# Grouping tokens by expert in the last layer of a four-layer conditional transformer, for three of four batches

## The chip, the cores and the metric

The kernel runs on one core of a Trainium2 chip. The metric is the device time of one launch in microseconds, the median of several runs. A profile of one execution gives the rows that this document reads.

## The reference

Four batches of N = 512 tokens, C = 288 channels, go through a rotation (layer L0, a matrix exponential) and then three transformer layers with 16 heads of 18 channels and a hidden width of FF = 1152. The first two have one MLP each. The last one has four experts; each token uses the two with the largest gate logits:

```python
xn = _modulate(_ln(x), sh_mlp, sc_mlp)
xf = xn.reshape(-1, C)
gate_logits = xf @ w_gate                                   # 288 x 4
topk_logits, topk_idx = jax.lax.top_k(gate_logits, TOP_K)   # TOP_K = 2
gates = jax.nn.softmax(topk_logits, axis=-1)
cw = jnp.sum(jax.nn.one_hot(topk_idx, NUM_EXPERTS, dtype=xf.dtype) * gates[..., None], axis=1)
hmid = jax.nn.gelu(jnp.einsum('tc,ech->eth', xf, w1) + b1[:, None, :], approximate=True)
eo = jnp.einsum('eth,ehc->etc', hmid, w2) + b2[:, None, :]
moe = jnp.einsum('te,etc->tc', cw, eo).reshape(B, N, C)
return x + g_mlp[:, None, :] * moe
```

As written, every expert computes every token, and `cw` is zero for the two that are not chosen.

## The kernel before

Everything is laid out by hand on one clock of *ticks* (`ticks()`, `TICKS`), the same list for all five engines. After an opening (rotation, conditioning vectors, a barrier `phase_over` for all engines) each layer has an attention stage of 16 steps of 8 ticks (`AT[l]`; step s holds four heads of batch s // 4, so 32 ticks a batch) and an MLP stage (`MT[l]`) of two ticks for each hidden tile. `items()` lists pieces of work as (tick, kind, layer, index, part); `agenda(engine)` hands each engine its list, moved by the offsets in `LAG` (POOL mostly one tick later). An engine runs its list strictly in order and waits on semaphores; a tick is an order, not a time. SP issues every DMA of the kernel, also in list order.

The MLP stage goes through *windows* of FT = 9 hidden tiles, a window being one batch under one expert. `hidden(l, s)` makes a tile of 128 hidden units for 512 tokens with `seven` matmuls (line 1696: the operands are split into a high part in fp32r and a low part, and seven products of chunks of 128 or 96 rows give full precision). `gelu_tile` (ACT, line 1556) writes `g32`, DVE splits it into `G` (lines 1322 and 1324), and `back` (line 1780) adds 12 matmuls for each tile into four PSUM banks. `finish` (DVE, lines 1143 to 1151) adds the bias, multiplies by the MLP's gate and, in the last layer, by the token's weight `cw` for the expert, and adds to `X`. G has three buffers, g32 two, the hidden tile's bank one; `back` of a tile runs two tiles behind its `hidden`. The last layer has 16 windows, expert by expert, four batches each.

Weights come in six *pieces* for each expert (three of w1, three of w2): `load_piece` on SP into one of two raw slots, `high_weights` on ACT (line 1354), `low_weights` on POOL (line 877). W1 and W2 of the experts alternate between two places. An expert's six pieces are spread over four windows.

The token's input to the MLP is made by `stats2` and `mean2` (DVE, then four small POOL instructions, lines 890 to 896), `scale` (ACT), and three `ln2` items: four transposes on PE into PSUM bank 7 (line 1820), two copies with scale and shift on ACT (lines 1519, 1520), the low part on POOL (line 928). Bank 7 is shared by all kinds in `ON_BANK`: each use waits until the one ahead has been read. `gate` makes the logits with 28 products of 4 columns, `choose` ranks them by six comparisons on DVE, `gexp` takes a power on POOL (line 969), `weigh` makes `cw`. In the last layer gates and choices stand in the first four windows. In attention each step ends with `out` (a transpose on DVE, then a product on POOL, line 933) and `turn` (a second transpose), each batch with four `proj` items (PE line 1844, DVE line 1272, an addition on POOL, line 939). Key scores are line 1735, their exponentials ACT's line 1545, values line 1749, query scores line 1717 and their maxima DVE's line 1133.

## Time and profile before

| | |
|---|---|
| median of 3 runs | 1902.89 us (1901.86 to 1903.12) |
| the profiled execution | 1896.54 us, its span 1894.1 us |
| granted TensorE clock, mean | 0.950 |
| PE busy | 1738.4 us (92%) |
| DVE, ACT, POOL busy | 1159.2, 914.4, 577.1 us |
| DMA | 116.49 MB, 61 GB/s over the span |

### The profile page before, as it was taken

How to read it: one execution, taken by the hardware profiler on the slowest of the kernel's cores; microseconds unless marked ns; L12 is line 12 of the kernel's file. 1: busy time of each engine (PE TensorE's matmuls, PEld its weight loads, DVE VectorE, ACT ScalarE, POOL GpSimd, SP SyncE). 2: the span in 40 equal slices, each digit the busy share in tenths (PEclk: the TensorE clock that was granted, in tenths of full speed). 3: DMA queues.
4: the chain of work that ended last, by engine and by line, in shares of the span. 5: the costliest groups of instructions: out<-in, count | busy, mean ns of one | idle time of the engine just before them, and what ended most of it. 6: DMA issues, size and time to landing. Idle time of an engine off the chain costs nothing.

```text
span 1894.1 us, 27931 instructions
## 1 busy us (share of the span) xinstructions
PE 1738.4 (92%) x9838; PEld 1141.3 (60%) x9838; DVE 1159.2 (61%) x2573; ACT 914.4 (48%) x1635; POOL 577.1 (30%) x567
## 2 busy tenths in 40 slices
PE   6775899998998889998899999999999999999998
PEld 2443444433796634443378764444388899999997
DVE  7863677773555667677436567777445645455454
ACT  2323476667354468675745247676733322222221
POOL 4432122214555323332435232222523301101000
PEclk9997699999999889899899999998999899999999
DMA  7202333331001222323100223333110000100000
GB/s 245 79 2 71 95 105 91 91 112 48 11 1 51 91 82 72 90 70 114 57 11 1 88 67 109 92 100 114 39 38 19 20 25 20 44 10 29 1 26 25
DMA packets 65866, 116.49 MB, mean 61 GB/s; under 512 B 9443, under 2 KB 25235, under 8 KB 65439
## 3 DMA queue, kind: packets, MB, share of 16 engines
q1 hardware_dynamic: 65728, 114.71, 19.6%
q8 instruction: 79, 1.29, 0.3%
q14 instruction: 59, 0.48, 0.1%
HBM read 83.46 MB, written 30.73 MB: 60 GB/s over the span
## 4 chain that ended last, share of the span: by engine, by line
PE 70%; DVE 10%; ACT 7%; issue 4%; DMA 4%; POOL 4%; SPq 2%; DVEq 0%; ACTq 0%; POOLq 0%
PE ps L1696 25%; PE ps L1780 15%; PE ps L1749 8%; PE ps L1735 7%; PE ps L1844 6%; PE ps L1717 5%; ACT Pr L1545 2%; DMA heads_t<-stage 2%; PE ps L1820 1%; DVE negmax L1133 1%; ACT HQ L1520 1%; DVE GT L1059 1%; ACT act L1519 1%; ACT xn L1441 1%; PE ps L1586 1%
## 5 line engine op out<-in xcount | busy, mean ns | idle before, releaser
L1133 DVE TENSOR_REDUCE negmax<-ps 128x1 f32<-128x512 f32 x768 | 488.3, 681 | 221.3 <-PE ps L1717 218.0
L1545 ACT ACTIVATE Pr<-ps 128x512 f32<-128x512 f32 x768 | 410.6, 602 | 208.3 <-PE ps L1735 208.0
L1556 ACT ACTIVATE g<-ps,b1col 128x512 f32<-128x512 f32 x216 | 148.2, 688 | 449.1 <-PE ps L1696 445.0
L1322 DVE CAST G<-g 128x512 fp32r<-128x512 f32 x216 | 122.8, 568 | 280.7 <-ACT g L1556 280.2
L1735 PE MATMUL ps<-QK 55*128 55x512 f32 x768 | 239.5, 515 | 33.4 <-ACT Pr L1545 25.2
L1780 PE MATMUL ps<-W2a,G 128*128 128x288 f32 x1728 | 263.4, 302 | 4.8 <-DVE rowt L1143 4.8
L1780 PEld LDWEIGHTS ps<-W2a,G 128*128 128x128 f32 x1728 | 247.9, 192 | 19.1 <-DVE G L1324 7.3
L1749 PE MATMUL ps<-Pr,V 128*32 128x512 f32 x1536 | 220.0, 646 | 0.0
L1717 PE MATMUL ps<-QK 54*128 54x512 f32 x768 | 196.6, 444 | 18.7 <-DVE negmax L1133 7.0
L1735 PEld LDWEIGHTS ps<-QK 55*128 55x128 f32 x768 | 92.2, 192 | 198.7 <-ACT Pr L1545 103.5
L1324 DVE TENSOR_TENSOR G<-g,G 128x512 fp32r<-128x512 f32 x216 | 170.4, 789 | 7.4
L1696 PE MATMUL ps<-HQ,W1a 128*128 128x512 f32 (+1 forms) x504 | 136.4, 411 | 7.4 <-ACT g L1556 5.9
L928 POOL TENSOR_TENSOR stage<-act,stage 126x512 fp32r<-126x512 f32 (+1 forms) x60 | 77.3, 1288 | 203.7 <-ACT stage L1537 165.1
L1780 PEld LDWEIGHTS ps<-W2b,G 128*128 128x128 f32 x864 | 123.5, 188 | 6.3
L1780 PE MATMUL ps<-W2b,G 128*128 128x288 f32 x864 | 126.9, 296 | 0.0
L1717 PEld LDWEIGHTS ps<-QK 54*128 54x128 f32 x768 | 96.1, 198 | 44.7 <-DVE negmax L1133 21.9
L1844 PE MATMUL ps<-WP,oT 128*128 128x288 f32 x384 | 121.1, 445 | 0.0
L928 POOL TENSOR_TENSOR HQ<-act,HQ 128x512 fp32r<-128x512 f32 (+1 forms) x54 | 69.6, 1288 | 136.3 <-ACT HQ L1520 123.1
L1696 PEld LDWEIGHTS ps<-HQ,W1a 128*128 128x128 f32 (+1 forms) x504 | 93.3, 194 | 28.9 <-ACT g L1556 8.2
L1844 PEld LDWEIGHTS ps<-WP,oT 128*128 128x128 f32 x384 | 70.1, 199 | 63.7 <-issue 31.0
L1696 PEld LDWEIGHTS ps<-WQ,HQ 128*128 128x128 f32 (+1 forms) x560 | 80.8, 197 | 41.9 <-issue 14.0
L1696 PE MATMUL ps<-WQ,HQ 128*128 128x288 f32 (+1 forms) x560 | 98.5, 317 | 7.9 <-ACT stage L1537 3.3
(221 smaller groups left out, 2241.1 us busy)
## 6 DMA issues: line engine op xcount, KB each, us to landing
QK<-heads_t SPq DMA_DIRECT2D x192, 144.0 KB
heads_t<-stage SPq DMA_DIRECT2D x96, 252.0 KB
QK<-heads_t SPq DMA_DIRECT2D x192, 72.0 KB
raw<-in_w SPq DMA_DIRECT2D x18, 432.0 KB
raw<-in_w SPq DMA_DIRECT2D x12, 576.0 KB
WA<-in_ada_w SPq DMA_DIRECT2D x3, 1728.0 KB
heads_t<-stage SPq DMA_DIRECT2D x24, 144.0 KB
QK<-W1a SPq DMA_DIRECT2D x192, 2.0 KB
```

What stands on the lines that cost most here:

```text
L928: pool.tensor_tensor(lo, act32[rows, h % 2, :], hi.bitcast(F32), ALU.subtract).then_inc(low_done, 1)
L1133: dve.tensor_reduce(negmax[:, m % 2, h, t:t + 1], ps[:, row_bank(l, s, i), :], AX, ALU.max, negate=True).then_inc(a_free, 1)
L1322: dve.tensor_copy(G[:, n % 3, 0, :], g32[:, n % 2, :]).then_inc(g_hi, 1)
L1324: dve.tensor_tensor(G[:, n % 3, 1, :], g32[:, n % 2, :], G[:, n % 3, 0, :].bitcast(F32), ALU.subtract).then_inc(g_lo, 1)
L1545: act.activation(Pr[:, t % 2, 2 * half + pair, :], ps[:, (16 * s + u) % 3, :], ACT.Exp, scale=SCALE).then_inc(b_free, 1)
L1556: act.activation(g32[:, n % 2, :], ps[:, hidden_bank(s), :], ACT.Gelu if l == 1 else ACT.Gelu_apprx_tanh, bias=b1col[:, e, s % FT:s % FT + ...
L1696: ins = mm(o, lhs(w, h, rows[w]), rhs(w, h, rows[w]), start=p == 0, stop=p == 6)
L1717: mm(ps[:, row_bank(l, s, i), :], QK[r:r + QROW, g, 0, pair, 128 * t:128 * t + 128], QK[r:r + QROW, g, 1, pair, :], start=True, stop=True) ...
L1735: mm(ps[:, k % 3, :], QK[r:r + QROW + 1, g, 1, pair, 128 * t:128 * t + 128], QK[r:r + QROW + 1, g, 0, pair, :], start=True, stop=True).the ...
L1749: ins = mm(ps[32 * i:32 * i + 32, 6, :], V[:, s // 4 % 2, t, c:c + 32], Pr[:, t % 2, i, :], start=t == 0, stop=t == TT - 1)
L1780: ins = mm(ps[:, t, 0:C], G[:, n % 3, x, 128 * t:128 * t + 128], W2[e % 2][:, w, ft, :], start=ft == 0 and p == 0, stop=ft == FT - 1 and p ...
L1844: ins = mm(bank[:, 0:C], oT[:, (STEPS * l + 4 * i + g) % 5, 128 * k:128 * k + 128], WP[:, g, :], start=g == 0, stop=g == 3)
```

## The change

In the last layer, the tokens of batches 0 to 2 (SEL = 3) are grouped by expert. Their modulated rows are written to DRAM (`tok_rows`, a region of 1536 rows for each expert) at the place that a running count gives them, twice each, once for each chosen expert. The windows then are tiles of 512 such rows: 3 x 512 x 2 = 3072 rows are six tiles, and rounding up for four experts makes at most GROUPED = 9. Which expert a tile belongs to is known at run time only (`table`, read by SP as register values), so every window loads all six pieces, and its bias rows, by a computed address. A tile is read back (`xg`), transposed (`lng`), and its result stored (`exp_rows`). At the end a gather fetches the two results of each token, and `merge` weights and adds them. The fourth batch is computed as before, under all four experts, in four more windows. `tok_rows` is filled with zeros in the opening. Core of the diff:

```diff
+LAST, SEL = LAYERS - 1, B - 1
+GROUPED = 2 * SEL + EXPERTS[-1] - 1
+WINDOWS = (B, B, GROUPED + EXPERTS[-1])
+REGION = SEL * N
+XROWS = (EXPERTS[-1] + 1) * REGION
+CW = C + 64
...
-        tiles = EXPERTS[l] * B * FT
+        tiles = WINDOWS[l] * FT
...
+def raw_slot(n):
+    return n % 2 if n < THREE else (n - THREE) % 3
...
+def choices(l, b):
+    if b == 1:
+        out += [(6, "setup", l, 0, 0), (12, "wg", l, 0, 0)]
+    if b == 2:
+        out += [(12 + t, "stats2", l, 0, t) for t in range(TT)] + [(17, "mean2", l, 0, 0)]
+        out += [(10, "modrow", l, 0, 0), (24, "mod", l, 0, 0)] + [(26 + c, "ln2", l, 0, c) for c in range(3)]
+        out += [(20 + t, "stats2", l, 1, t) for t in range(TT)] + [(26, "mean2", l, 1, 0), (28, "modrow", l, 1, 0)]
+        out += [(29, "gate", l, 0, 0), (31, "gturn", l, 0, 0), (33, "gexp", l, 0, 0), (34, "rank", l, 0, 0), (35, "weigh", l, 0, 0)]
+        out += [(36, "scatter", l, 0, 0)]
+    if b == 3:
+        out += [(2 + c, "ln2", l, 1, c) for c in range(3)] + [(11, "mod", l, 1, 0)]
+        out += [(13, "gate", l, 1, 0), (15, "gturn", l, 1, 0), (17, "gexp", l, 1, 0), (18, "rank", l, 1, 0), (19, "weigh", l, 1, 0)]
+        out += [(20, "scatter", l, 1, 0)]
+        out += [(t, "stats2", l, 2, k) for k, t in enumerate((8, 10, 12, 14))] + [(14, "mean2", l, 2, 0), (14, "modrow", l, 2, 0)]
+        out += [(19, "mod", l, 2, 0)] + [(19 + c, "ln2", l, 2, c) for c in range(3)]
+        out += [(22, "gate", l, 2, 0), (24, "gturn", l, 2, 0), (26, "gexp", l, 2, 0), (26, "rank", l, 2, 0), (27, "weigh", l, 2, 0)]
+        out += [(27, "scatter", l, 2, 0), (27, "table", l, 0, 0), (30, "xg", l, 0, 0)]
+        first = PIECE["w1", l, 0, 0]
+        out += [(t, "load", l, first + q, 0) for q, t in enumerate((0, 0, 5, 9, 13, 26))]
+        out += [(t, "split", l, first + q, 0) for q, t in enumerate((4, 7, 10, 25, 31, 32))]
...
+def grouped_window(l, v):
     out = [(4, "fin", l, v - 1, 0)] if v > 0 else []
+    if 0 < v <= GROUPED:
+        out += [(5, "store", l, v - 1, 0)]
     if v == 0:
+        out += [(0, "out", l, STEPS - 1, 0), (0, "turn", l, STEPS - 1, 0)]
+        out += [(0, "proj", l, B - 1, t) for t in range(TT)]
+        out += [(0, "lng", l, 0, c) for c in range(3)] + [(6, "slots", l, 0, 0), (2, "b2", l, 0, 0)]
+    if v == 1:
+        out += [(t // 2, "stats2", l, B - 1, t) for t in range(TT)] + [(2, "mean2", l, B - 1, 0)]
+        out += [(8 + c, "ln2", l, B - 1, c) for c in range(3)]
+    if v == 2:
+        out += [(2, "gate", l, B - 1, 0), (4, "gturn", l, B - 1, 0), (6, "gexp", l, B - 1, 0), (9, "weigh", l, B - 1, 0)]
+    if v == 4:
+        out += [(3, "gates", l, 0, 0)]
+    if v + 1 < WINDOWS[l]:
+        first = PIECE["w1", l, v + 1, 0]
+        out += [(t, "load", l, first + q, 0) for q, t in enumerate((-3, -2, -1, 8, 10, 12) if v > 0 else (2, 2, 3, 8, 10, 12))]
+        out += [(t, "split", l, first + q, 0) for q, t in enumerate((5, 7, 9, 12, 14, 16))]
+        out += [(9, "side", l, v + 1, 0)]
+    if v + 1 < GROUPED:
+        out += [(1, "xg", l, v + 1, 0)] + [(11 + 2 * c, "lng", l, v + 1, c) for c in range(3)]
+    for b in range(SEL):
+        if v == GROUPED + b:
+            out += [(8, "gather", l, b, 0), (14, "merge", l, b, 0), (16, "merge", l, b, 1)]
...
+            sp.dma_start(tok_rows.rearrange("(k p) c -> p k c", p=128),
+                         act32[:, 0, 0:CW].unsqueeze(1).broadcast_to([128, XROWS // 128, CW])).then_inc(zero_out, 16)
...
+            sp.wait_ge(zero_out, 16)
             phase_end(sp)
...
+                elif kind == "scatter":
+                    pool.wait_ge(zero_out, 16)
+                    pool.wait_ge(mod_done, i + 1)
+                    pool.wait_ge(idx_ready, i + 1)
+                    for t in range(TT):
+                        for r in range(2):
+                            pool.indirect_dma_start(tok_rows, bass.IndirectOffsetOnAxis(idx[:, i, t, r:r + 1], 0),
+                                                    MB[i // 2][:, t, :], None).then_inc(xs_out, 16)
+                    pool.wait_ge(xs_out, 16 * 2 * TT * (i + 1))
+                elif kind == "gather":
+                    pool.wait_ge(ys_out, 16 * GROUPED)
+                    pool.wait_ge(slots_ready, 1)
...
+                    for t in range(TT):
+                        for r in range(2):
+                            pool.indirect_dma_start(XG[r][:, t, 0:C], None, exp_rows,
+                                                    bass.IndirectOffsetOnAxis(yidx[:, i, t, r:r + 1], 0)).then_inc(yg_in, 16)
+                    pool.wait_ge(yg_in, 16 * 2 * TT * (i + 1))
...
+                dve.tensor_tensor(mb[:, :, :], xn[:, :, :], bc3(modr[:, 1, :], TT), ALU.mult).then_inc(dve_done, 1)
+                dve.wait_ge(dve_done, step())
+                dve.tensor_tensor(mb[:, :, :], mb[:, :, :], bc3(modr[:, 0, :], TT), ALU.add).then_inc(mod_done, 1)
...
-                    for t in range(TT):
-                        ins = seven(bank[:, 4 * t:4 * t + 4], lambda w, h, r: x[0:r, h, 128 * t:128 * t + 128],
-                                    lambda w, h, r: Wg[0:r, w, :], KROWS)
+                    ins = seven(bank[0:4], lambda w, h, r: Wg[0:r, w, :], lambda w, h, r: x[0:r, h, :], KROWS)
...
+                late = (what, l, s, u) == ("m", LAST, 0, 0)
+                if what == "m" and u == 0 and (EARLY if l < LAST else 0) <= s < tiles and not late:
                     hidden(l, s)
...
                 for key in todo[tick]:
                     work(*key)
+                if late:
+                    hidden(l, s)
```

Not shown: `rank` (ranks of the tokens in their regions, a dozen small instructions on DVE behind two or three narrow matmuls), `table` and `slots` (some 20 and 13 small DVE instructions, once each), `gturn` (four narrow matmuls), `merge` (8 + 2 DVE instructions), the SP functions for `xg`, `store`, `side`, `modrow` and `gates`, and the waits that each new reuse of a buffer needs. `lng` is like `ln2` with plain copies.

## Rows read from the trace of the kernel before

**Rows 1.** Stretches: busy us of PE, PEld, DVE, ACT, POOL; clock; DMA share, GB/s.

```profile
1253.00:1313.00 60.00, 57.69 (x323) 25.77 (x319) 44.73 (x77) 36.94 (x71) 12.76 (x12) 1.00 0.28 86
1313.00:1377.00 64.00, 59.01 (x282) 23.92 (x282) 31.48 (x61) 45.84 (x87) 27.61 (x25) 0.89 0.21 64
1377.00:1533.00 156.00, 147.87 (x827) 129.40 (x826) 80.77 (x224) 51.44 (x76) 49.45 (x36) 0.91 0.09 30
...
1538.50:1567.60 29.10, 29.10 (x172) 26.26 (x172) 14.63 (x27) 6.19 (x9) 0.00 (x0) 1.00 0.00 1
```

**Rows 2.** POOL's timeline (start, length in us, engine, line, operation): one split, four windows apart.

```profile
1577.15 3.02 POOL L877 TENSOR_TENSOR W1a<-raw,W1a 128x1152 fp32r<-128x1152 f32 x1 [46.56 <-ACT W1a L1354]
...
1693.48 3.02 POOL L877 TENSOR_TENSOR W1b<-raw,W1b 128x1152 fp32r<-128x1152 f32 x1 [46.56 <-ACT W1b L1354]
```

**Rows 3.** Timeline of the last window: its last hidden tile, and its end.

```profile
1880.42 1.77 PE L1696 MATMUL ps<-HMw,W1b 128*128 128x512 f32 x7
...
1887.50 1.36 DVE L1148 TENSOR_TENSOR rowt<-rowt,gbc 128x1152 f32<-128x1152 f32 x1
```

**Rows 4.** End of attention, and the projection behind it, in the timeline.

```profile
1378.03 1.07 PE L1749 MATMUL ps<-Pr,V 128*32 128x512 f32 x8
...
1382.09 1.05 POOL L933 TENSOR_TENSOR oTok<-oTok,rsum 128x512 f32<-128x512 f32 x1 [10.59 <-DVE rsum L1250]
...
1388.63 2.10 PE L1844 MATMUL ps<-WP,oT 128*128 128x288 f32 x8
...
1390.87 0.46 DVE L1272 TENSOR_TENSOR ptmp<-ps,agate 128x288 f32<-128x288 f32 x1 [3.11 <-PE ps L1844]
...
1391.48 0.81 POOL L939 TENSOR_TENSOR X<-X,ptmp 128x288 f32<-128x288 f32 x1 [2.58 <-DVE ptmp L1272]
```

**Rows 5.** Timeline and clock around the third choice of experts.

```profile
1462.69 3.80 PE L1696 MATMUL ps<-Wg,HQ 128*128 128x4 f32 x28
...
1467.00:1471.00 4.00, 3.11 (x9) 0.50 0.00 0
```

**Rows 6.** The last transposes before a window, and what the window waits for.

```profile
1493.40 0.60 PE L1820 MATMUL ps<-ident,xn 128*96 128x128 f32 x4
...
1497.06 1.87 PE L1696 MATMUL ps<-HMw,W1a 128*128 128x512 f32 x7 [1.48 <-POOL HMw L928]
...
1491.00:1495.00 4.00, 4.00 (x28) 1.00 0.35 113
```

**Rows 7.** Part of one choice of experts on DVE, in the timeline.

```profile
1426.07 0.54 DVE L1171 TENSOR_TENSOR wins<-lg 128x4 f32<-128x4 f32 x6
```

**Rows 8.** The opening: last early load, first instruction behind the barrier, DMA rate.

```profile
70.06 0.28 SPq L687 DMA_DIRECT2D raw<-in_b_qkv  x1
...
133.87 0.52 POOL L906 MEMSET HQ<- 2x512 f32 x1 [6.62 <-ACTq L597]
...
10.00:20.00 10.00, 5.08 (x44) 2.05 (x44) 7.63 (x44) 1.80 (x6) 3.91 (x6) 1.00 1.06 303
```

**Rows 9.** Groups of instructions from 1360 us to the end.

```profile
L877 POOL TENSOR_TENSOR W1b<-raw,W1b 128x1152 fp32r<-128x1152 f32 (+1 forms) x6 | 16.7, 2787 | 85.1 <-ACT W1b L1354 85.0
L877 POOL TENSOR_TENSOR W2b<-raw,W2b 128x864 fp32r<-128x864 f32 x6 | 12.7, 2121 | 46.4 <-ACT W2b L1354 46.3
L969 POOL TENSOR_TENSOR tmp<-euler,tmp 128x16 f32<-128x16 f32 x4 | 12.4, 3110 | 36.1 <-DVE tmp L1167 36.1
...
L928 POOL TENSOR_TENSOR HQ<-act,HQ 128x512 fp32r<-128x512 f32 (+1 forms) x6 | 7.7, 1286 | 9.5 <-ACT HQ L1520 9.3
...
L1519 ACT ACTIVATE act<-ps,ada 128x512 f32<-128x512 f32 (+1 forms) x12 | 9.5, 788 | 11.0 <-PE ps L1820 11.0
```

**Rows 10.** Landing of the output's transfers, from the DMA view.

```profile
out<-X SPq DMA_DIRECT2D x4, 576.0 KB, 3.0
```

**Rows 11.** A split of weights on POOL beside a cast on DVE.

```profile
1448.84 2.67 POOL L877 TENSOR_TENSOR W1b<-raw,W1b 128x1152 fp32r<-128x1152 f32 x1
...
1449.73 2.07 DVE L1322 CAST G<-g 128x512 fp32r<-128x512 f32 x1 [2.98 <-ACT g L1556]
```

More of the change, by code:

```diff
@@ L288 @@
 LAG = {
[L289 to L290 removed]
+    "PE": dict(ym=0, l0=0, ln1=0, ln2=0, qk=0, tok=0, v=0, max=0, proj=0, gate=0, gturn=0, rank=0, lng=0, warm=0),
+    "ACT": dict(ym=0, scale=0, root=1, ln1=0, ln2=0, lng=0, gate=0, qk=0, tok=0, max=0, split=0, bias=0, wg=0),
     "DVE": dict(add=0, inverse=0, stats1=0, stats2=0, mean1=0, mean2=0, v=0, proj=0, out=0, turn=0, warm=0, var=0, root=0, centre=0, fin=0,
[L292 to L293 removed]
+                gturn=0, weigh=0, rank=0, table=0, slots=0, merge=0, mod=0),
+    "POOL": dict(gexp=0, setup=0, scatter=0, gather=0, mean1=1, mean2=1, ln1=1, ln2=1, lng=1, qk=1, out=1, proj=1, tok=1, root=3, split=1, centre=1, fin=1, wg=1,
                  ones=0, vones=0),
[L295 removed]
+    "SP": dict(onerow=0, qk=2, max=1, place=0, load=0, wp=0, agate=0, mlpc=0, b2=0,
+               modrow=0, xg=0, store=0, side=0, gates=0),
 }
@@ L1845, in work @@
                                  start=g == 0, stop=g == 3)
+                elif kind == "gturn":
+                    pe.wait_ge(misc_free, MISC["gate", l, i, 0] + 1)
+                    for t in range(TT):
+                        ins = mm(bank[:, 4 * t:4 * t + 4], lgT[:, 128 * t:128 * t + 128], ident[0:4, 0:4], start=True, stop=True)
                 else:
```

554 lines of the change are left out of this document (438 added, 116 removed).

## The prediction

> **What bounds the kernel now.** I read the cores' clock and the forty slices of the page first: PE is busy through the whole last layer. Then busy time by stretch [rows 1]. In attention for the last layer's batches 2 and 3 (1253 to 1377 us) PE is busy 116.7 of 124 us; DVE is at 75% and then 49%, POOL at 21% and 43%. From 1377 to 1533 PE still has 148 of 156 us, and from there each window (nine hidden tiles and their products back, for one batch and one expert) is PE alone: 29.1 busy of 29.1 us. The POOL timeline gives the period: the same weight split of two experts, four windows apart, stands 116.33 us apart, so 29.1 us a window [rows 2]. The last window begins eight tiles of 3.23 us ahead of its last hidden tile at 1880.42, at 1854.6; its final scaling starts at 1887.50 [rows 3], 32.9 us after the window's start, and 6.6 us before the span's end at 1894.1. Attention ends with the last values product at 1379.1 [rows 4]. From there to 1854.6 are 475.5 us for 15 windows, which at 29.1 are 436.5: 39 us go to the projection of batch 3, transposes, four gates and slow clock. One such place is the third gate: 28 products of 4 columns take 3.80 us and the clock behind them is granted at 0.50, 1.2 GHz instead of 2.4 [rows 5].
>
> **What it removes.** Sixteen windows become 9 grouped and 4 dense: three fewer, 3 x 29.1 = 87 us of pure PE time, and the count is fixed in the program, so that this part cannot fail to happen. The gates of 28 narrow products, with their slow clock, go too.
>
> **Attention, +27 us.** I measure it to its last values product. The two hidden tiles that lay inside it leave: -3 (two of 1.77 us [rows 3]). For each of three batches PE gets 12 transposes (1.8 us [rows 6]), 7 gate products of full width (1.8, as a hidden tile [rows 3]), 16 narrow ones for turning and ranking (1), 4.6 in all. DVE gets a choice (six comparisons take 0.54 us [rows 7]; some 22 such instructions and six waits, 2.3), a ranking of a dozen (2), statistics (2) and two passes of 1408 elements for the modulation, at 1.36 us for 1152 [rows 3] 1.65 each: 10 us. In the second half of batch 2, DVE already has 22 of 30 us: +7 us, of which 4.6 are PE's. In batch 3 POOL sets the pace. A scatter is 8 indirect transfers, and POOL then waits until they land. No row shows an indirect transfer. Bounds: SP's issue of a plain one, 0.28 us [rows 8], and POOL's longest small instruction, the power at 3.11 [rows 9]; I take 1.1, as a POOL instruction on 128 rows takes 1.05 [rows 4]. With landing at 3.0 [rows 10] a scatter holds POOL 8 x 1.1 + 3 = 12 us (bounds 5 and 28). From tick 4 to the gate of batch 2 at tick 22 POOL has, in its order: scatter 12; three W1 lows 8.4; four low parts of ln2 5.2 [rows 9]; four additions of the projection 3.2, two oTok products 2.1 [rows 4]; the small statistics 2; one power 3.1; the second scatter 12: 48 us. DVE and POOL hinder each other: a cast that started under a split on POOL ran 2.07 us and ended only behind it [rows 11]; 5 more. The gate on PE waits for the low parts queued behind the second scatter, and PE's queue, the key scores with it, stands behind the gate. 18 ticks of 64/32 = 2.0 us are 36: 53 - 36 = +17. Behind it gate, turn and rank on PE, exposed with few scores beside them: +3 and, for DVE's choice ahead of the rank, +3.
>
> The Trainium skill (DMA: Bandwidth & Descriptors, Anatomy of one DMA — SWDGE (gpsimd) path) has a fixed 2.0 us and bytes at 436 GB/s for a transfer of this path, 2.3 us for one of 180 KB; by that, an estimate, a group would end 0.7 us sooner and the six groups 4 us in all. No row here shows one.
>
> **The gap, 31 us.** Window 0's hidden tile now stands behind everything of its tick. Scatter 2 starts some 11 us behind gate 2 and ends at 23; two W2 lows (4.2) and the oTok product come behind it, at 28.5, while attention ends some 18 us behind that gate: 10 us late. Then the turn 0.7; four projections, each half of 2.10, 0.46 on DVE and hand-offs, 1.9 x 4 = 7.6 [rows 4]; three groups of transposes through one bank, 0.6 [rows 6] + 2 x 0.79 on ACT [rows 9] + 0.2, 7.1; a low part 1.3; and 4 for a clock at 0.50 once PE has idled, as [rows 5] shows behind light work. Bounds 20 and 45.
>
> **Windows, +24, +10, +9 us.** Eight windows hold 12 transposes more, 1.8 us. The last low part must be there when the next window begins: before, with transposes one tick later, PE waited 1.48 us [rows 6]; now a W2 low (2.1 [rows 9]) can stand ahead of it. I take 1.2 (bounds 0 and 3.6): 8 x 3.0 = 24. Each window now splits six pieces: 3 x 2.79 + 3 x 2.12 = 14.7 us, low parts 3.9, on POOL, and DVE, busy for 14.6 in a window [rows 1], has some 10 us of casts and differences that get in POOL's way: 28.6 of 32, it fits without much room. ACT needs 6.2 more of 32. Weights and tiles are 4.3 MB a window, 137 GB/s, under half the 303 that rows show [rows 8]: hidden. Batch 3's ln2, its gate and the scales of windows 1 and 2 are 10. Windows 9 to 11 each hold a gather of 12 us on POOL between two W1 lows; the piece of W2 whose slot the late low frees comes 8 us late, ACT waits for it ahead of the next gelu, and DVE's merge waits for the gather. A tile's G is ready some 2 us behind the tile and used two tiles, 6.5 us, behind it: against that slack of 4.5, 3 a window: 9 (bounds 0 and 45). Stores, side loads and table reads are SP's, with windows of time: nothing; if a table read blocked SP for 3 us, the W2 loads' 6 us lead would still cover it.
>
> **The opening, 0.** 7680 rows of 1408 bytes, 10.8 MB, are zeroed behind the last early load at 70.3, and SP's barrier waits for them; the barrier opens at 133.9 [rows 8]. That is 63.6 us, enough from 170 GB/s on. The opening's rate was 303, attention's 86 [rows 1]; I take 200. Bounds 0 and 62.
>
> **The sum.** 1379.1 + 27 + 31 = 1437.1; 12 x 29.1 = 349.2; + 24 + 10 + 9: the last window begins at 1829.3; + 32.9 + 6.6 = 1868.8, against 1894.1: 25 us less. The profiled execution took 1896.5 (its span and 2.4 around it), 6 us under the median of the runs, 1902.9; I put the difference on that: 1902.9 - 25 = 1878 us.
>
> **Rivals.** (a) The groups hide. If an indirect transfer costs POOL what it costs SP, a group is 5 us; POOL catches up in attention (+9), the gap is 21, transposes alone remain (14), windows 1 and 2 cost 7 and gathers nothing: 1379.1 + 9 + 21 + 349.2 + 14 + 7 + 39.5 = 1818.8, 75 less: 1828 us. POOL's 21 and 43% of busy time speak for it, the pile of splits and scatters in batch 3 against.
> (b) Slower: POOL's price for an indirect transfer. Eight of them count in two scatters, the late third and three gathers, 48 us for each us of price. It decides from 1.1 + 25/48 = 1.6 us on; at 2.2 it is +53, 1931 us. The 3.11 us for a power on 16 elements [rows 9] speaks for it, POOL's 1.05 us for 512 elements against.
> (c) The zeros at attention's rate: 62 us later, 1940.
> (d) The clock. The stretch that held the last transposes before a window was granted 1.00 [rows 6]. If the clock fell instead in each grouped window for some 8 us, as it does behind a gate of narrow products, at half speed that would be 4 us in each of eight windows: 1878 + 32 = 1910. The Trainium skill (TensorE: Matmul & The Clock Gate, Part 4: PE-mode transpose) says that transposes do not count as PE being busy as other matmuls do; by that rule (d) would come, and the trace does not bear it out.
>
> **Chances.** My forecast 0.53 (its own range 1848 to 1900), (a) 0.15, (b) 0.18, (c) 0.04, (d) 0.04, and 0.06 that extra waits eat the gain to within some us of nothing. A measurement here can tell 0.2%, 3.8 us. Faster: 0.53 + 0.15 + 0.02; slower: 0.18 + 0.04 + 0.03 for half of (d) and a share of the last; same 0.05. The range runs from (a) to short of (b)'s middle: 1828 to 1915; it leaves out the far half of (b), (c) and a little below (a).
>
> **What would show it.** In the profile of the changed kernel: POOL's time per indirect transfer (1.1 us) and per group (12); PE's wait at batch 2's gate for POOL's low part (over 8 us); about 31 us from the last values product to the first hidden tile; a grouped window of 32 us, a dense one 29 to 32; the first instruction behind the barrier still near 134; the clock at 1.00 in grouped windows. Wrong it is made above all by the price of an indirect transfer, by a barrier later than 140, or by ACT held at a W2 piece in every window.

## The result, and the profile after

The changed kernel takes 1927.2 us (median of four runs), the kernel before 1902.4: a ratio of 1.013, 95% interval 1.010 to 1.016. The forecast was 1878 us, 1828 to 1915. The profiled execution's span is 1920.3 us, 26.2 more than before, where 25 less were forecast: 51.5 us to account for.

The windows view of the changed kernel: attention from the ninth step's maximum to the last values product, in two parts; the gap to the first hidden tile; window 0 up to its first bias addition; windows 1 to 8; windows 9 to 11.

```profile
1249.40:1301.20 51.80, 51.80 (x288) 23.60 (x284) 39.89 (x77) 32.71 (x63) 13.46 (x16) 1.00 0.30 91
1301.20:1436.60 135.40, 101.50 (x426) 40.71 (x422) 71.72 (x218) 67.96 (x123) 66.63 (x57) 0.71 0.24 76
1436.60:1468.30 31.70, 15.03 (x44) 9.26 (x44) 3.51 (x7) 3.25 (x6) 13.04 (x12) 0.66 0.35 110
1468.30:1510.90 42.60, 39.03 (x199) 33.45 (x200) 28.15 (x42) 17.70 (x24) 20.62 (x11) 0.88 0.27 81
1510.90:1763.50 252.60, 248.97 (x1481) 222.14 (x1480) 173.67 (x202) 124.11 (x174) 155.67 (x76) 1.00 0.45 139
1763.50:1887.50 124.00, 99.74 (x515) 87.11 (x514) 91.56 (x108) 35.73 (x45) 67.06 (x42) 0.88 0.37 110
```

Up to 1301 hardly anything has changed (51.5 us before). Then the stretch that took 78.3 us takes 135.4: PE's busy time is up from 71.0 to 101.5, its idle time from 7.3 to 33.9, and the mean clock is down from 0.91 to 0.71. Grouped windows run at the full clock (1.00), as [rows 6] had it. Windows 9 to 11 take 124 us where three windows at 29.1 [rows 2] are 87: PE is idle for 24.3, and the same products take 99.7 us at a mean clock of 0.88.

What PE waits for in the second of these stretches (releaser: us in total, times, longest):

```profile
PE ps L2141 <- issue: 13.6, 2, 11.3
PE ps L2162 <- DVE negmax L1384: 9.1, 5, 2.7
PE ps L2194 <- DVE oTok L1647: 4.5, 2, 2.3
```

The timeline around the first of these, the gate of batch 2, then attention's end and the projection (start, length, engine, line, operation, idle time before it and what ended it):

```profile
1402.59 0.96 POOL L1203 DMA_INDIRECT tok_rows<-MB,idx  x1 [0.30 <-issue]
1405.17 2.59 POOL L1144 TENSOR_TENSOR HQ<-act,HQ 128x512 fp32r<-128x512 f32 x2 [1.62 <-DMA tok_rows<-MB,idx]
...
1407.86 3.15 PE L2141 MATMUL ps<-HQ,Wg 128*4 128x512 f32 x7 [11.27 <-issue]
...
1434.63 1.93 PE L2194 MATMUL ps<-Pr,V 128*32 128x512 f32 x8 [1.18 <-ACT Pr L1984]
1445.68 4.18 PE L2307 MATMUL ps<-WP,oT 128*128 128x288 f32 x8 [9.12 <-DVE oT L1655]
...
1468.34 3.36 PE L2141 MATMUL ps<-HQ,W1a 128*128 128x512 f32 x7 [2.62 <-POOL HQ L1144]
```

POOL issues the last transfers of batch 1's scatter, waits 1.62 us for them to land, and only then makes the low parts that the gate product needs: the gate has stood for 11.27 us and every key score behind it. An indirect transfer costs 0.96 + 0.30 us, a scatter 11.5 to 12.6 us with its landing (1.1 and 12 forecast). From 1400.2 to 1454.8 the clock is at 0.50, its lower level of 1.2 GHz: a values product takes 1.93 us and the projection 4.18, where [rows 4] has 1.07 and 2.10; the first window's hidden tiles take 3.36 against 1.77 [rows 3].

Window 9, on POOL and DVE:

```profile
1785.14 2.80 POOL L1093 TENSOR_TENSOR W1a<-WP,W1a 32x1152 fp32r<-32x1152 f32 x1 [1.93 <-DMA XG<-exp_rows,yidx]
1788.02 4.12 POOL L1093 TENSOR_TENSOR W2a<-raw,W2a 128x864 fp32r<-128x864 f32 x2
1792.34 2.00 POOL L1093 TENSOR_TENSOR W2a<-WP,W2a 128x864 fp32r<-128x864 f32 x1 [0.21 <-ACT W2a L1765]
1808.34 2.71 POOL L1093 TENSOR_TENSOR W1b<-raw,W1b 128x1152 fp32r<-128x1152 f32 x1 [14.00 <-ACT W1b L1765]
1811.56 2.73 POOL L1093 TENSOR_TENSOR W1b<-raw,W1b 128x1152 fp32r<-128x1152 f32 x1 [0.51 <-ACT W1b L1765]
...
1785.09 7.21 DVE L1422 TENSOR_SCALAR XG<-XG,cws 128x288 f32<-128x288 f32 x4 [5.29 <-DMA XG<-exp_rows,yidx]
1792.34 3.61 DVE L1426 SCALAR_TENSOR_TENSOR XG<-XG,cws,XG 128x288 f32<-128x288 f32 x4
...
1808.00 6.62 DVE L1408 SCALAR_TENSOR_TENSOR X<-rowt,cw,X 128x288 f32<-128x288 f32 x4
```

The gather holds the low parts back; the merge waits 5.29 us for it at the head of DVE's queue, and both then start together. DVE's four scalings take 7.21 us and end at 1792.30, 0.16 behind POOL's two W2 low parts; the finish's four accumulations take 6.62 and end at 1814.62, 0.33 behind its second W1 part. Experiment 3 shows such four beside an idle POOL at 1.81. PE waits 21.4 us for G in these windows, in five pieces.

### The profile page after: what moved, and what is told of

Read it like the earlier page. It is cut to its first block, busy times and chain, and to the rows that moved or that the text cites. A ratio compares the mean times of both kernels' runs of the same rounds, so it can differ in the third digit from the quotient of the medians.

```text
span 1920.3 us, 27798 instructions
## 1 busy us (share of the span) xinstructions
PE 1697.5 (88%) x9395; PEld 1079.3 (56%) x9395; DVE 1236.0 (64%) x2552; ACT 978.1 (51%) x1720; POOL 794.4 (41%) x713
## 4 chain that ended last, share of the span: by engine, by line
PE 59%; DVE 12%; ACT 8%; POOL 8%; issue 6%; DMA 4%; SPq 2%; another core or an unknown queue 0%; DVEq 0%; ACTq 0%; POOLq 0%
PE ps L2141 20%; PE ps L2229 10%; PE ps L2194 8%; PE ps L2180 7%; PE ps L2307 6%; PE ps L2162 4%; DMA heads_t<-stage 2%; ACT Pr L1984 2%; DVE negmax L1384 2%; PE ps L2283 1%; POOL W2a L1093 1%; DVE XG L1422 1%; POOL HQ L1144 1%; DVE GT L1310 1%; ACT HQ L1959 1%
## 5 line engine op out<-in xcount | busy, mean ns | idle before, releaser
L1997 ACT ACTIVATE g<-ps,b1col 128x512 f32<-128x512 f32 x189 | 129.7, 687 | 318.1 <-PE ps L2141 283.9
L1731 DVE CAST G<-g 128x512 fp32r<-128x512 f32 x189 | 142.4, 754 | 205.5 <-ACT g L1997 195.4
L2180 PE MATMUL ps<-QK 55*128 55x512 f32 x768 | 241.5, 528 | 26.5 <-ACT Pr L1984 18.3
L2229 PE MATMUL ps<-W2a,G 128*128 128x288 f32 x1620 | 245.1, 301 | 8.1 <-DVE G L1733 7.5
L2229 PEld LDWEIGHTS ps<-W2a,G 128*128 128x128 f32 x1620 | 231.7, 191 | 21.4 <-DVE G L1733 10.0
L2162 PE MATMUL ps<-QK 54*128 54x512 f32 x768 | 199.7, 447 | 29.3 <-DVE negmax L1384 16.2
L2141 PE MATMUL ps<-HQ,W1a 128*128 128x512 f32 (+1 forms) x693 | 189.6, 414 | 15.2 <-ACT g L1997 8.9
L1733 DVE TENSOR_TENSOR G<-g,G 128x512 fp32r<-128x512 f32 x189 | 194.6, 1030 | 6.5
L2180 PEld LDWEIGHTS ps<-QK 55*128 55x128 f32 x768 | 93.1, 196 | 186.3 <-ACT Pr L1984 91.1
L2141 PEld LDWEIGHTS ps<-HQ,W1a 128*128 128x128 f32 (+1 forms) x693 | 129.9, 197 | 45.7 <-ACT g L1997 12.6
L1144 POOL TENSOR_TENSOR HQ<-act,HQ 128x512 fp32r<-128x512 f32 (+1 forms) x69 | 90.8, 1315 | 142.0 <-ACT HQ L1959 117.6
L2307 PE MATMUL ps<-WP,oT 128*128 128x288 f32 x384 | 126.3, 461 | 11.5 <-DVE oT L1655 9.1
L2162 PEld LDWEIGHTS ps<-QK 54*128 54x128 f32 x768 | 96.6, 200 | 57.2 <-DVE negmax L1384 33.9
L2229 PE MATMUL ps<-W2b,G 128*128 128x288 f32 x648 | 98.8, 303 | 13.9 <-DVE G L1733 13.9
L1149 POOL TENSOR_TENSOR oTok<-oTok,rsum 128x512 f32<-128x512 f32 x48 | 50.8, 1059 | 140.9 <-DVE rsum L1649 140.0
L2229 PEld LDWEIGHTS ps<-W2b,G 128*128 128x128 f32 x648 | 94.8, 194 | 20.5 <-DVE G L1733 15.9
## 6 DMA issues: line engine op xcount, KB each, us to landing
tok_rows<-act SPq DMA_DIRECT2D x1, 10560.0 KB, 34.5
```

The costliest lines, as they stand in the source:

```text
L1144: pool.tensor_tensor(lo, act32[rows, h % 2, :], hi.bitcast(F32), ALU.subtract).then_inc(low_done, 1)
L1731: dve.tensor_copy(G[:, n % 3, 0, :], g32[:, n % 2, :]).then_inc(g_hi, 1)
L1733: dve.tensor_tensor(G[:, n % 3, 1, :], g32[:, n % 2, :], G[:, n % 3, 0, :].bitcast(F32), ALU.subtract).then_inc(g_lo, 1)
L1997: act.activation(g32[:, n % 2, :], ps[:, hidden_bank(l, s), :], ACT.Gelu if l == 1 else ACT.Gelu_apprx_tanh, bias=b1col[:, v % 4 if l == L ...
L2141: ins = mm(o, lhs(w, h, rows[w]), rhs(w, h, rows[w]), start=p == 0, stop=p == 6)
L2162: mm(ps[:, row_bank(l, s, i), :], QK[r:r + QROW, g, 0, pair, 128 * t:128 * t + 128], QK[r:r + QROW, g, 1, pair, :], start=True, stop=True) ...
```

## The experiments

All are variants of the changed kernel. Beside them the kernel before was run again, on four chips: medians of 1898 to 1902 us, and each ratio is against these runs. What lies ahead of attention's last part is the same code in all of them and still ends up to 14 us apart, so stretches are compared inside each execution: **attention** is from the ninth step's maximum to the last values product (before 129.8, changed 187.2), the **gap** from there to the first hidden tile (changed 31.8), **windows 9 to 12** from the first bias addition of window 8 to that of the last (changed 148.5; the last four before 111.7). Each stretch is read from one execution. The seven kernels with the change's attention (the change, 3 to 6, 8 and 9) took 185.5 to 190.9 us for it, so a difference under some 3 us there says nothing; the gap was 31.8 in six of them.

**1. Batch 1's scatter two steps later.**

```diff
-        out += [(20, "scatter", l, 1, 0)]
+        out += [(22, "scatter", l, 1, 0)]
```

> The change with one edit: batch 1's scatter, whose eight indirect transfers hold GpSimd for 12.6 us, is queued two steps later, behind the low parts that batch 2's gate product waits for. Theory 1 (the new queue order on GpSimd): TensorE no longer waits 11.3 us before that gate product, its clock does not fall to 0.50 around it, attention's last values product comes 15 to 25 us earlier than 1436.6, the gap after it and the first window (both run at half clock in the change) get shorter by another 5 to 15 us, and the whole is 1895 to 1905 us. Theory 2 (attention is late because VectorE is overloaded by the choices' small operations): the wait moves from GpSimd to VectorE's row maxima, the end of attention moves by less than 5 us and the whole stays at 1920 to 1927.

Measured: 1917.9 us, 1.0094 [1.0064, 1.0124]. The wait of 11.3 us is gone, attention takes 182.1: 5 us less. Its clock is still 0.81 on average (0.79 in the change), and PE now waits for DVE:

```profile
PE ps L2162 <- DVE negmax L1384: 11.6, 5, 3.7
PE ps L2194 <- DVE oTok L1647: 4.8, 1, 4.8
```

Theory 1 falls as the main cause; theory 2 is nearer, though the wait is real.

**2. One transfer of eight in a scatter.**

```diff
-                    for t in range(TT):
-                        for r in range(2):
+                    for t in range(1):
+                        for r in range(1):
                             pool.indirect_dma_start(tok_rows, ...
```

> The change with only the first of the eight indirect transfers of each scatter issued, so seven eighths of the tokens' rows are left out of the grouped computation; everything else, the zero fill and all the loads among it, stays. GpSimd is free 10.5 us earlier at each of the three scatters. Theory 1 (GpSimd's occupation by the scatters sets attention's end): last values product near 1410 instead of 1436.6, the gap of 31.8 us shorter by 3 to 6 us because the sixth W2 low part and the last output's scaling come sooner, whole 1888 to 1900. Theory 2 (VectorE's load): end of attention near 1430, whole 1918 to 1925. Windows 9 to 11 are as in the change under both, 41 us each.

Measured: 1914.1 us, 1.0060 [1.0024, 1.0095]; attention 174.7, gap 27.7. Eighteen us less of POOL's time in attention gave 12.5, half of what theory 1 wanted, and more than theory 2 allowed.

**3. Gather at step 17, merge at steps 2 and 3 of the next window.**

```diff
-            out += [(8, "gather", l, b, 0), (14, "merge", l, b, 0), (16, "merge", l, b, 1)]
+            out += [(17, "gather", l, b, 0)]
+        if v == GROUPED + b + 1:
+            out += [(2, "merge", l, b, 0), (3, "merge", l, b, 1)]
```

> The change with the three gathers issued from the seventeenth step of their window, behind the window's last low part, in place of the eighth, and the merges at steps 2 and 3 of the next window, ahead of its first low part. Theory 3 (in windows 9 to 11 GpSimd's twelve microseconds for a gather push the low parts back, and the merge then collides with them): windows 9 to 12 take 120 to 128 us in place of 148.5, whole 1898 to 1908. Rival (the merge's own arithmetic on VectorE, 7 to 9 us of it a window beside G's, is what the windows are longer by): 136 to 146 us, whole 1915 to 1924. Attention and the gap stay as in the change.

Measured: 1949.3 us, 1.0231 [1.0163, 1.0300], windows 9 to 12 163.9. Neither held, because I had put the merge ahead of the finish (step 4) that frees PSUM. DVE waits for the gather at the head of its queue (32.5 us in the three windows), and PE for DVE:

```profile
1816.83 3.56 DVE L1424 TENSOR_SCALAR XG<-XG,cws 128x288 f32<-128x288 f32 x4 [10.95 <-DMA XG<-exp_rows,yidx]
...
1829.09 1.81 DVE L1410 SCALAR_TENSOR_TENSOR X<-rowt,cw,X 128x288 f32<-128x288 f32 x4
```

**4. No weighting in the merge.** Nine of its ten operations are gone.

> The change with the merges' weighting left out: the gathered rows of the first choice are added to X as they are, the two scalings by the choice's weights, the second choice's rows and the product with the gate row are left out (of ten VectorE operations a merge one stays). Gathers and their places stay. Theory 3 (GpSimd's occupation by the gather decides): windows 9 to 12 take 138 to 146 us in place of 148.5, whole 1917 to 1925. Rival (the merge's arithmetic on VectorE decides): windows 9 to 12 take 118 to 126 us, whole 1897 to 1907.

Measured: 1915.6 us, 1.0076 [1.0043, 1.0108]; windows 9 to 12 132.3. That is 16.2 us less for 3 x 5 us of unhindered work, between the two expectations: the merge decides nearly half of the excess.

**5. Merge at steps 9 and 11 of the next window**, gather as in 3.

> The change with each gather issued from step 17 of its window, as in the third experiment, but the merges at steps 9 and 11 of the next window, behind the finish of step 4, so that VectorE never waits for a gather in front of the bias additions that free PSUM. Theory 4 (an SBUF operation of VectorE starts only between GpSimd's big operations, and a gather waited for at the head of VectorE's queue stops everything behind it; the third experiment was slower because TensorE waited 16 us three times for the bias additions): windows 9 to 12 take 120 to 138 us in place of 148.5 (163.9 in the third experiment), and the merge's ten operations still take 8 to 14 us in windows 10 and 11, but about 6 in window 12, where GpSimd has no low parts. Rival (the gathers' time on GpSimd alone decides): 142 us or more.

Measured: 1915.8 us, 1.0067 [1.0033, 1.0101]; windows 9 to 12 128.3. The scalings still took 18.5 us for twelve where they met low parts.

**6. Low parts of 64 columns for windows 3 to 12.**

```diff
+                if PIECES[n][0] == "w2" and PIECES[n][2] >= 3:
+                    lo, part, high = lo[:, 0, 0:64], part[:, 0, 0:64], high[:, 0, 0:64]
+                elif PIECES[n][0] == "w1" and PIECES[n][2] >= 3:
+                    lo, part, high = lo[:, 0:64], part[:, 0:64], high[:, 0:64]
```

> The change with GpSimd's low parts of the weights cut to 64 columns for windows 3 to 12 of the last layer (the other columns of the low part are left as they were, so the last bits of these products are not computed); high parts, gathers and merges stay. Theory 4 (VectorE's operations wait for GpSimd's): windows 9 to 12 take 115 to 125 us in place of 148.5, the merge's four scalings take 1.5 us in place of 7.2, the last window's four accumulations 1.8 in place of 6.6; windows 4 to 8 go from 31.0 to 29.1. Rival (the gather's landing and VectorE's own work decide): windows 9 to 12 stay above 136 us, windows 4 to 8 at 31.0.

Measured: 1895.8 us, 0.9977 [0.9934, 1.0019]; windows 9 to 12 114.5, with gathers and merges where the change has them. The groups of DVE in these windows, of the change and then of this kernel (count, busy us, mean ns of one, idle before):

```profile
L1422 DVE TENSOR_SCALAR XG<-XG,cws 128x288 f32<-128x288 f32 x12 | 19.4, 1673 | 5.3 <-DMA XG<-exp_rows,yidx 5.3
L1408 DVE SCALAR_TENSOR_TENSOR X<-rowt,cw,X 128x288 f32<-128x288 f32 x12 | 15.0, 1314 | 0.1
L1731 DVE CAST G<-g 128x512 fp32r<-128x512 f32 x34 | 18.3, 538 | 35.8 <-ACT g L1997 26.4 <-issue 9.2
```

```profile
L1426 DVE TENSOR_SCALAR XG<-XG,cws 128x288 f32<-128x288 f32 x12 | 4.7, 454 | 9.7 <-DMA XG<-exp_rows,yidx 9.7
L1412 DVE SCALAR_TENSOR_TENSOR X<-rowt,cw,X 128x288 f32<-128x288 f32 x12 | 5.6, 529 | 0.1
L1735 DVE CAST G<-g 128x512 fp32r<-128x512 f32 x34 | 14.4, 425 | 30.6 <-ACT g L2001 30.4
```

The same twelve scalings take 4.7 us in place of 19.4, though DVE now waits longer for the gathers (9.7 us) than before. The gathers' time alone costs next to nothing. The edit frees POOL as well as DVE; what PE waited for in the change's windows 9 to 11 was DVE's G (21.4 us), and no wait there is put down to POOL. Windows 4 to 8 went only from 31.0 to 30.4: of the 1.9 us over 29.1, 1.3 stay with the transposes and 0.6 were POOL's (in the change PE waits 0.3 us in such a window for the late low part).

**7. Less choosing on DVE** (for batches 1 and 2 the comparisons are skipped, batch 1 is modulated for one tile of four).

> The change with less of the choices' work on VectorE: for batches 1 and 2 the twenty small operations that find the chosen experts are left out (batch 0's choices are used again), and the modulated rows of batch 1 are made for one tile of four. That is some 6 us less of 72 us of VectorE's work in the last batch of attention. If VectorE's load is what makes TensorE wait and its clock fall, attention's last values product comes 12 to 25 us sooner, counted from the ninth step's maximum (187 us in the change, 130 before). If it is GpSimd's queue, it comes less than 5 us sooner.

Measured: 1918.1 us, 1.0077 [1.0048, 1.0105]; attention 178.4, mean clock 0.85. Six us of DVE's work were worth 9, between the two; the gate's wait of 11.4 is still there. PE's idle time did not change (34.3 us for 33.9): the 9 us came back as busy time (144.1 for 153.3) at the higher clock.

**8. Eight idle products on PE behind attention's last.**

```diff
+                    if l == LAST:
+                        filler(8)    # mm(ps[:, 5, 0:288], ident, V[:, 1, 0, 0:288])
```

> The change with eight products of 128 by 288 that compute nothing used, queued on TensorE behind attention's last values product, where it waits 9.1 us for VectorE and GpSimd. If the half clock of the projections and of the first window comes from TensorE's idle time just before, the projections take 2.1 to 2.3 us in place of 4.18, and from the last values product to the first window's first bias addition it takes 60 to 66 us in place of 74.4. If the clock does not depend on it, or the fillers only hold the projections up, 74 to 79 us. Everything ahead and behind is as in the change.

Measured: 1932.1 us (two runs), 1.0150 [1.0036, 1.0265]; from the last values product to the first bias addition 73.6 us (74.4 in the change). The clock rose at 1446.0 and fell again at 1452.8: the first projection took 2.84 us in place of 4.18, the second 4.21 as before. The gain that was expected did not come. Between the fillers and the first projection PE still waited 3.19 us for DVE, and 0.65 behind it; which pause brought the clock down again is not shown.

**9. Merges and finishes in two-operand forms.**

```diff
-                    for t in range(TT):
-                        dve.tensor_scalar(XG[0][:, t, 0:C], XG[0][:, t, 0:C], cws[:, b, t, 0:1], None, ALU.mult)...
+                    for r in range(2):
+                        y = XG[r][:, :, 0:C]
+                        dve.tensor_tensor(y, y, cws[:, b, :, r:r + 1].broadcast_to([128, TT, C]), ALU.mult)...
```

> The change with the merges and the finishes of windows 9 to 12 written in two-operand operations alone: a tile's scaling by a column (four operations with a scalar for each tile) becomes one product of 128 by 1152 with that column broadcast, and one sum. Order, places and gathers stay. In the change, in windows 9 to 12, VectorE's operations of those forms were 29.0 us longer than their shortest ones in sum (those of L1422 15.8, of L1408 9.7, of L1426 3.5), while the two-operand ones of L1405, L1433 and L1435 kept their 1.35 us. Theory 5 (only the forms with a scalar operand and the one-operand casts wait for GpSimd's operation in flight): windows 9 to 12 take 122 to 134 us in place of 148.5. Rival (every form waits; the long two-operand ones only happened to run beside an idle GpSimd): 144 to 154 us, and the new products take 2 to 4 us each.

Measured: 1935.8 us (two runs), 1.0171 [1.0119, 1.0222]; windows 9 to 12 152.3. Theory 5 falls. Two groups of this kernel, the merge's product and the finish's:

```profile
L1423 DVE TENSOR_TENSOR XG<-XG,cws 128x1152 f32<-128x1152 f32 x6 | 17.1, 2891 | 6.0 <-DMA XG<-exp_rows,yidx 6.0
...
L1408 DVE TENSOR_TENSOR rowt<-rowt,cw 128x1152 f32<-128x1152 f32 x3 | 4.1, 1358 | 0.1
```

The same product takes 2.89 us in the merge and 1.36 in the finish. The form doesn't matter, the neighbour does, and who came first: two of the finish's three products began 0.35 and 0.63 us ahead of a low part, kept their 1.36, and the low part took 3.54 and 3.27 us in place of 2.7. The sum behind each began inside the low part and took 3.7.

**10. Scatter as in 1, the table behind the last output's transpose, the last output scaled by DVE.**

```diff
-        out += [(0, "out", l, STEPS - 1, 0), (0, "turn", l, STEPS - 1, 0)]
+        out += [(0, "out", l, STEPS - 1, 0), (0, "table", l, 0, 0), (0, "turn", l, STEPS - 1, 0)]
```

> The change with three moves out of GpSimd's and VectorE's queues in attention's last stretch: batch 1's scatter two steps later as in the first experiment; the table of the windows' starts (4.2 us of small operations on VectorE before attention's end) made after the last output's transpose; and the last output's scaling done by VectorE, where it stood on GpSimd behind the third scatter and two low parts (7.2 us of VectorE's wait at 1437.6). Theory: the gap of 31.8 us becomes 24 to 28, attention's last values product comes 5 to 12 us sooner after the ninth step's maximum than the 187 us of the change, whole 1903 to 1913. Rival (GpSimd's low parts and the clock bound the gap, VectorE's table was hidden): gap 30 to 32, attention 182 to 184, whole 1916 to 1922.

Measured: 1916.8 us, 1.0081 [1.0049, 1.0113]; attention 177.1, gap 30.3. Attention did better than the rival said, the gap and the whole as the rival said; experiment 16 tells why the gap did.

**11 and 12. The moves of 10 and 5 together**, with the forms of 9 and with the old ones.

> The change with the moves of the tenth experiment, the gathers and merges of the fifth (gather at step 17, merge at steps 9 and 11 of the next window) and the two-operand forms of the ninth. If the gains add, 187 minus 5 to 12 for attention, gap 24 to 28, windows 9 to 12 120 to 128 us: whole 1878 to 1895 us, 0.99 to 1.00 of the kernel before. If attention's clock gives the gains back, 1895 to 1905.

> The eleventh experiment with the merges and finishes in their old forms (one operation with a scalar for each tile). If the forms did not matter, or the broadcast products cost a little more: windows 9 to 12 128 us (130.5 in the eleventh, 128.3 in the fifth), attention 177 to 179 us from the ninth step's maximum, gap 30, whole 1893 to 1899 us.

Measured: 1898.0 us, 0.9979 [0.9948, 1.0010], and 1897.6 us, 0.9977 [0.9947, 1.0008]; windows 9 to 12 130.5 and 128.3, attention 178.5 and 177.9, gap 30.3 in both. The gains of 5 and 10 add. The whole lies where the second expectation of 11 had it, level with the kernel before, because the gap had not shrunk; 12 came as expected.

**13. Low parts in thirds.**

> The twelfth with GpSimd's low parts of the weights for windows 2 to 12 made in three operations of a third each (384 columns, or one block of 288) in place of one. Theory 4 (an SBUF operation of VectorE waits for the one that GpSimd has in flight): the longest wait falls from 2.5 us to about 1, so VectorE gets in more often; windows 9 to 12 120 to 126 us in place of 128, whole 3 to 8 us less than the twelfth. Rival (only the sum of GpSimd's time counts, and it grows by some fixed cost for each operation): 128 to 133 us, no gain or a loss.

Measured: 1909.0 us, 1.0026 [0.9995, 1.0058]. The longest wait of a scaling fell from 2.5 us to 0.9, but windows 9 to 12 took 127.3 and windows 1 to 8 262.6 in place of 252.6. The rival holds: shorter waits, as long a sum (DVE is busy for 91.1 us of windows 9 to 12, 92.4 in experiment 12), and more work for POOL (78.9 us for 70.7).

**14. The cuts of 2 and 7 on top of 12.**

> The twelfth with the cuts of the second and of the seventh experiment together: one of eight transfers a scatter, the twenty choosing operations of batches 1 and 2 and three quarters of batch 1's modulation left out. If attention's lateness is VectorE's load, GpSimd's occupation and the clock that falls with TensorE's waits, and nothing else, from the ninth step's maximum to the last values product it takes 150 to 163 us (187 in the change, 177 in the tenth, 130 before). If something else makes TensorE late (its own added work, the spills), it stays at 168 or more.

Measured: 1884.7 us, 0.9893 [0.9847, 0.9938]; attention 162.3, mean clock 0.87. It is at the upper end of what the loads should explain: 25 of the 57 us. PE is busy for 142.5 us of it, 122.5 before. Of the 32.5 us that are left over the kernel before, 12.5 are idle time of PE and 20.0 busy time; by groups the added products, less the hidden tiles and the old gate, are 16 of the 20.

**15. The modulated rows made by GpSimd**, on top of 12.

> The twelfth with the three batches' modulated rows made by GpSimd in place of VectorE: 12.8 us less on VectorE in attention's last stretch, 16 to 20 more on GpSimd. If VectorE's load decides, attention takes 165 to 173 us from the ninth step's maximum in place of 177 to 179, whole 1885 to 1893. If GpSimd's queue decides as much (two operations of 2.7 to 3.5 us each ahead of the low parts), 177 to 188 us, whole 1895 to 1908.

Measured: 1889.6 us, 0.9945 [0.9919, 0.9971]; attention 174.7. For attention this is less than the first expectation gave and better than the second; the whole is in the first one's range. DVE and POOL at step 18 of batch 3:

```profile
1385.70 3.16 POOL L1129 TENSOR_TENSOR MB<-xn,modr 128x1408 f32<-128x1408 f32 x1 [0.29 <-ACT xn L1868]
1388.93 3.21 POOL L1131 TENSOR_TENSOR MB<-MB,modr 128x1408 f32<-128x1408 f32 x1
```

```profile
1387.11 1.78 DVE L1467 TENSOR_SCALAR pen<-chosen 128x16 f32<-128x16 f32 x1
1388.92 3.25 DVE L1471 TENSOR_TENSOR seen<-place_in,pen 128x16 f32<-128x16 f32 x2
```

An operation on 16 elements takes 1.78 us and ends within 0.04 us of POOL's; the next two take 3.25 and end with POOL's second. At 1413.08 to 1413.37, beside POOL's power on 16 elements, the latter two take 0.29.

**16 and 17. The table behind the turn; then gathers and merges moved away from low parts.**

```diff
+            out += [((17, 21, 0)[b], "gather", l, b, 0)] if b < 2 else []
+        if (v, b) == (GROUPED + 1, 0):
+            out += [(17, "merge", l, 0, 0), (18, "merge", l, 0, 1)]
+        if (v, b) == (GROUPED + 3, 1):
+            out += [(1, "merge", l, 1, 0), (3, "merge", l, 1, 1)]
+        if (v, b) == (GROUPED + 3, 2):
+            out += [(5, "gather", l, 2, 0), (15, "merge", l, 2, 0), (16, "merge", l, 2, 1)]
```

> The fifteenth with the table made after the last output's turn in place of ahead of it. In the fifteenth VectorE had the output scaled at 1426.2 and began its turn only at 1433.4, behind the table's small operations, three of which took 1.9 to 2.2 us beside GpSimd's two low parts. Theory: the table's 4 to 7 us now lie beside the first projection (4.0 us), the gap of 30.1 us becomes 23 to 27, whole 1881 to 1887, 0.990 to 0.993 of the kernel before. Rival: the table holds the first projection's product with the gate row up by what it held the turn up before, the gap stays at 28 to 30.

> The sixteenth with gathers and merges moved to where GpSimd has no low parts in flight: gather of batch 0 at step 17 of window 9, its merge at steps 17 and 18 of window 10, gather of batch 1 behind it (it lasts into window 11 and holds that window's low parts up by some 8 us), its merge at steps 1 and 3 of the last window, which has no low parts, gather of batch 2 at step 5 and its merge at 15 and 16. Theory 4 (merges are slow only beside low parts): windows 9 to 12 take 116 to 122 us in place of 128, whole 6 to 12 us less than the sixteenth. Rival: the low parts held up in window 11 make TensorE wait at the start of window 12, or the last merge comes late to the end: 124 to 132 us, no gain.

Measured: 1890.4 us, 0.9959 [0.9933, 0.9984], gap 27.7; and 1888.7 us, 0.9934 [0.9911, 0.9957], gap 27.7 and windows 9 to 12 124.9. In 16 the last output's turn starts 1.8 us behind its transpose (in 15 8.9 us), but the table, beside the two low parts, now ends at 1439.25; the second projection waits 3.29 us for it and then takes 4.21 us in place of 2.21, at the lower clock: two thirds of the 7 us are lost again. Its gap is just under the rival's range, its whole above what was expected. In 17 windows 9 to 12 came as the rival said, with 1.7 us less in all where 6 to 12 were expected. The merge's scalings are down to 5.4 us for twelve, but the low parts have moved onto G's casts instead (26.0 us for 34, 18.3 in the change):

```profile
L1744 DVE CAST G<-g 128x512 fp32r<-128x512 f32 x34 | 26.0, 766 | 25.6 <-ACT g L2010 25.4
...
L1446 DVE TENSOR_SCALAR XG<-XG,cws 128x288 f32<-128x288 f32 x12 | 5.4, 512 | 0.0
```

It is the fastest of those that compute everything: 0.7% under the kernel before, some 2% under the change by the two ratios. The intervals of 15, 16 and 17 overlap.

## Why the prediction was wrong

The miss by place: attention 30.5 us (57.5 for +27), the gap 0.8, window 0 6.6 (42.6 from its first hidden tile to its first bias addition; in the kernel before, the window before the last begins at 1825.5 and has its at 1861.5, 36.0), windows 1 to 8 14.2 the other way, windows 9 to 12 27.8 (148.5 less 111.7 is 36.8, for 9). The two large ones have causes of their own.

**"Windows, ... +9": the gathers' term, mis-sized (36.8 us for 9).** I had weighed the late W2 piece against PE's slack and let the merge wait for the gather. What I left out is the merge and the finish themselves beside the low parts. I had the row for it, [rows 11], and used it for attention ("5 more"); for the windows I added DVE's work to POOL's and found that "it fits" in POOL's 32 us, without asking the same of DVE. While POOL subtracts a piece of weights, DVE's casts, scalings and two-input operations on SBUF wait for its end. In a window, by [rows 9] and [rows 1], 14.7 us of POOL's pieces and some 10 of DVE's casts and differences already exclude each other for 25 of 29 us; the finish adds 3.2 and a merge 6.1 (experiment 6), and the window overflows. That sum, 34 us, tells that it overflows and not by how much: of the 36.8 us, 24.3 are PE's idle time and 12.4 the same products at a clock of 0.88. Experiment 6 shows the cause: with small pieces the excess goes from 36.8 us to 2.8 with every gather and merge in place. The Trainium skill (SBUF — State Buffer, Who interferes with whom) says this of a VectorE operation in a two-port mode or with two SBUF inputs against a GpSimd one that reads SBUF: an exclusive lock, held for the whole instruction, for whoever comes first. These rows agree for POOL's subtractions, sums and products, with 1.78 us for 16 elements and 1.67 in place of 0.45 for a scaling. They do not for its power, which held no operation of DVE's (last section); there the measurement decides. I had cited nothing of it in the prediction, where it would have named the missing sum. Experiment 9 shows that it is not the form, 13 that it is not the length of one piece, and 4, 5 and 17 give back 16 to 24 us by taking merges out or away from the pieces.

**"Attention, +27": a bound left out.** The chain that I named is there: POOL 11.3 us late at batch 2's gate, scatters of 12 us (12 forecast), and PE's queue stands behind it. But it was not the bound: with the wait gone (experiment 1) PE waits for DVE's row maxima and output transposes, and 5 us come back. I had counted DVE's 10 us a batch in the second half of batch 2, and for batch 3 only POOL's, as if POOL were full; from 1345 to the gate it was idle for 10.6 us for DVE alone (5.6 for the projection, 5.0 for the statistics). There DVE's work went from 42.6 to 71.7 us, nearly all of the 78.3 that the stretch had taken, in one queue with the maxima for which PE waits. Then the clock: I gave it 4 us in the gap and none in attention. PE, which had waited 7 us, waited 34, and the clock's mean over attention went from 0.95 of 129.8 us to 0.79 of 187.2. So the 57.4 us are 26.6 of idle PE and 30.8 of busy PE. Of the busy time some 20 are the added products by their groups (transposes 9.1 for 2.0, gates 9.1, turns 4.0, ranks 4.2, less 3.8 for the hidden tiles and 0.4 for the old gate), where the forecast's 4.6 a batch less 3 is 10.8; a gate of 1.8 us took up to 3.15 at the lower level. The other 10 are mostly the same products more often at half clock (the 260 values products 43.4 us for 37.3, the 94 query products 24.2 for 21.2). Shown by runs: the gate's wait (5 us), the scatters (12.5), DVE's work (9), both with the moves (25). The other 32 are read from experiment 14's rows (16 added products, 4 the same ones, 12.5 waits) and not taken away by any run. What brings the clock down stays open too: experiment 7 had as much idle time as the change and a mean of 0.85 for 0.79, and experiment 8's attempt in the gap gained nothing.

**Rival (d)** had its place wrong: grouped windows stay at 1.00. The clock falls where PE has waits, in attention's end, the gap, window 0 and windows 9 to 11 (0.88).

**"The gap, 31 us"**: 31.8, right in sum and in part by luck. POOL's oTok product comes at 1443.74 behind the third scatter and two W2 low parts, as forecast; PE waits 9.1 us where 10.7 were forecast, the projections take longer at half clock, 4.8 us twice and 2.8 twice (15.3 for 11.6 with the clock's 4), and the transposes with the low part less (7.4 for 8.4). Window 0 then takes 6.6 us too many, with 0.88 as its mean clock and hidden tiles of 3.36 us at its start: I had no term for it.

**"Eight windows, +24" and "+10"**: 19.8 for 34; with 31.0 us a window the transposes cost 1.3 for 1.8 and the late low part 0.6 for 1.2, by experiment 6. **The opening, 0**, right: 10.8 MB of zeros landed 34.5 us after their issue at 70.4, and the first instruction behind the barrier stood at 133.9, as before [rows 8]. **Rival (b)** did not come: 1.26 us for a transfer against the 1.6 from which it decides. That a scatter took the forecast's 12 us is luck in part: a transfer cost more than 1.1, and the wait behind the last one 1.6 to 2.0 us where I had 3.0. (The estimate of 2.3 us for 180 KB that stands there is 2.4 by the two figures given with it; no term rested on it.) The 87 us for three windows less came in full, and were spent.

## What to carry to other kernels

Work that lies "hidden" on two engines must be added up for both together where they exclude each other; each alone had seemed to fit. When a wait goes, ask what was 5 us behind it in another queue, and try the next two before crediting the first with everything. And put a number on the clock wherever the change makes the matrix engine wait repeatedly: here attention got 27 us of waits, and some 10 more by the same products at the lower level; windows 9 to 11 got 24 and 12.
